# Cross attention with 16 heads: maxima rows issued by ScalarE, key side by half heads of two pairs, value products alternating between column halves, context loads one group nearer

## The chip, the core and the metric

The kernel runs on one core of one Trainium2 chip. The core has five engines that run side by side and meet only at semaphores: TensorE (PE; matmuls), VectorE (DVE), ScalarE (ACT), GpSimd (POOL) and SyncE (SP; here it only starts transfers). Transfers run on 16 DMA engines. The metric is the device time of one execution in microseconds; the median of three runs counts.

## The reference

`x` and `ctx_1024` are 128 batches of 64 rows of 128 numbers. One layer is computed, all of it in float32:

```
x = x + xattn(layernorm(x), ctx, ctx)
      q, k, v = rows @ W.T + b, 16 heads of 8 numbers
      scores  = q . k / sqrt(8), softmax over the 64 keys, times v, then @ Wo.T + bo
x = x + ffn(layernorm(x))
      two gates (out, in): grouped conv of 4 columns, batch norm over all 8192 rows, gelu, linear to 128,
      softmax, the 32 largest of 128 kept
      out = (x @ W) * gate_out + (x * gate_in) @ W + bias
```

## The kernel before

**Two phases.** The batch norm needs all rows, so the kernel first does the attention and the grouped convolution of everything (phase 1), and then the gates' top 32 and the two products (phase 2, 16 groups, VectorE busy nearly throughout). The change touches phase 1 and the start.

**Phase 1** works on 16 groups of 4 pairs of batches. It is a software pipeline: in step t of the loop `for t in range(FIRST, LAST + 1)` (t from -3 to 17), each engine works on group t+3 (layer norm), t+2 (keys and queries projected), t (row maxima), t-1 (softmax and value products, output projection) and t-2 (residual, second layer norm, convolution). Each engine has its own hand-written list for one step; they are coupled by counting semaphores.

**Scores with 96 rows.** A float32 score is computed as a bf16 matmul over 2 x 48 rows: q and k are split in three bf16 parts (`split_queries` on VectorE, `split_keys` on GpSimd), written to DRAM (`write_parts`, L228, 4 transfers a group) and read back stacked (`stack`, L240, 12 transfers a group, into `kst` and `qst`).

- `query_side` (L338) multiplies with the queries on the output rows; VectorE takes the maxima over the keys (`row_max`, L678). 16 heads in 8 calls a group; its matmuls alternate between the two column halves of the array (64 columns of weights each).
- The maxima are split in two bf16 parts, turned by PE (`turn_max`, L351), copied by ACT (`max_out`, L544, into `mT`), and written by a transfer into four more rows of `qst` (`max_rows`, L247). There are two such transfers a group, one for each half hp (two pairs).
- `key_side` (L291) multiplies again with the keys on the output rows, over 100 rows, so the maximum is already subtracted; ACT takes the exponential (`exp_half`, L511) into `pT`. It can only start when the maxima rows of its half have landed. Before, a call is one pair p with all 16 heads, 8 into each of two PSUM banks.
- `values` (L305) takes `pT` as weights (128 x 64 float32) and 18 columns of V with a column of ones. Each float32 matmul shows as two passes in the trace, so one call is 32 passes. Before, a call is one pair p, and all 32 passes go to the column half pp = p % 2.

**SP's list of one step, before:** `max_rows(t-1, 1)`; load x of t+5; load the context of t+4 (L205), which waits until PE has used the buffer, that is until `values_in(t)` (L373) is done; then wait for all key sides of t-1 and issue `stack(t+1)` for keys and queries (L240); write the parts of the keys of t+2; `max_rows(t, 0)`; write the parts of the queries of t+2. SP is a strict list: what stands behind a wait is late with it.

## Time and profile before

| | us |
|---|---|
| median of 3 runs | 907.33 (898.88 to 907.83) |
| profiled execution | 896.31, its span 894.5 |
| PE busy / weight loads | 642.7 / 509.5 |
| VectorE busy | 469.2 |
| ScalarE busy | 362.1 |
| GpSimd busy | 283.8 |
| mean granted TensorE clock | 0.608 of full speed |

Phase 1 ends near 650 us. In the page's 40 slices PE is busy six to nine tenths over most of phase 1, VectorE two to four; from slice 29 on VectorE stands at nine. How to read it: a step's length in phase 1 is the distance between the first key-side matmuls of two neighbouring groups. "Idle before" names who ended an engine's wait.

### The profile page before, as it was taken

What the parts mean: (1) busy time and instruction counts of PE and PEld (TensorE: products, weight loads), DVE (VectorE), ACT (ScalarE), POOL (GpSimd) and SP (SyncE); (2) the same over time, 40 slices, a digit from 0 to 9 for tenths busy, and PEclk for the clock granted to TensorE, in tenths of its full rate; (3) what the DMA queues carried; (4) which work ended last, traced back from release to release, by engine and by line L of the source; (5) the groups of instructions that cost most, each with busy time, mean ns of one, the idle gap of its engine ahead of it and who ended that gap; (6) DMA issues with size and microseconds to landing.
All of it is one profiled execution on the core that took longest, in us unless ns stands there. A gap on an engine that the chain in (4) does not pass through costs nothing.

```text
span 894.5 us, 15479 instructions
## 1 busy us (share of the span) xinstructions
PE 642.7 (72%) x5186; PEld 509.5 (57%) x5186; DVE 469.2 (52%) x2214; ACT 362.1 (40%) x995; POOL 283.8 (32%) x352
## 2 busy tenths in 40 slices
PE   2348695976969788796976999999466666575742
PEld 0126584765847566585755778887345545454531
DVE  7241333423334233323423354432399999999993
ACT  2213232323424234232323443333576565656563
POOL 4522031230302303031230321000135656565665
PEclk9655567657766557556666696656555555555555
DMA  5751506426164251605326344400000000000000
GB/s 119 167 103 39 122 23 118 75 58 115 31 118 66 67 95 39 131 14 119 62 59 117 59 77 87 73 2 2 1 1 25 12 25 12 25 13 24 22 15 25
DMA packets 64942, 52.70 MB, mean 59 GB/s; under 512 B 6805, under 2 KB 57174, under 8 KB 63318
## 3 DMA queue, kind: packets, MB, share of 16 engines
q1 hardware_dynamic: 64862, 51.70, 28.0%
q8 instruction: 42, 0.69, 0.3%
q14 instruction: 38, 0.31, 0.1%
HBM read 34.38 MB, written 16.78 MB: 57 GB/s over the span
## 4 chain that ended last, share of the span: by engine, by line
PE 40%; DVE 27%; DMA 13%; SPq 12%; issue 3%; ACT 3%; POOL 1%; POOLq 0%; ACTq 0%; DVEq 0%
PE ps_pv L305 15%; DVE kst L790 14%; DMA qst<-mT 12%; SPq L240 10%; DVE top_next L781 8%; PE ps_col L291 6%; PE ps_row L338 5%; PE ps_proj L373 3%; PE ps_proj L366 3%; DVE top_first L781 3%; PE ps_proj L360 2%; PE ps_mix L324 2%; SPq L228 1%; ACT gates L606 1%; DMA qst<-q_scratch 1%
## 5 line engine op out<-in xcount | busy, mean ns | idle before, releaser
L305 PEld LDWEIGHTS ps_pv<-vx,pT 128*64 128x64 f32 x2048 | 180.0, 186 | 18.5 <-issue 17.4
L305 PE MATMUL ps_pv<-vx,pT 128*64 128x18 f32 x2048 | 181.7, 243 | 0.2 <-DVE attn L696 0.2
L678 DVE TENSOR_REDUCE m<-ps_row 128x8 f32<-128x512 f32 x128 | 85.5, 690 | 174.9 <-PE ps_row L338 174.6
L803 POOL TENSOR_SCALAR ve<-ag 128x4 f32<-128x4 f32 x32 | 7.3, 227 | 454.9 <-DVE ag L670 453.8
L511 ACT ACTIVATE pT<-ps_col 128x512 f32<-128x512 f32 x128 | 69.5, 594 | 182.3 <-PE ps_col L291 181.5
L291 PE MATMUL ps_col<-qst,kst 100*128 100x64 bf16 x1024 | 60.5, 226 | 98.8 <-DMA qst<-mT 96.8
L291 PEld LDWEIGHTS ps_col<-qst,kst 100*128 100x128 bf16 x1024 | 50.8, 125 | 111.0 <-DMA qst<-mT 100.2
L790 DVE MATCH_REPLACE8 kst<-top_next,kst 128x128 f32<-128x128 f32 x384 | 101.1, 280 | 0.0
L338 PE MATMUL ps_row<-kst,qst 96*64 96x128 bf16 x1024 | 80.2, 297 | 9.5 <-DMA qst<-q_scratch 8.5
L338 PEld LDWEIGHTS ps_row<-kst,qst 96*64 96x64 bf16 x1024 | 55.0, 140 | 42.5 <-issue 25.8
L781 DVE MAX8 top_next<-kst 128x8 f32<-128x128 f32 x384 | 78.1, 279 | 0.0
L704 DVE TENSOR_TENSOR xr<-xr,ps_mix 128x256 f32<-128x256 f32 x32 | 13.4, 420 | 111.1 <-PE ps_mix L324 111.1
L485 PE MATMUL ps_proj<-wf_sb,x2T 128*128 128x128 f32 x128 | 33.2, 441 | 49.1 <-ACT x2T L624 49.1
L485 PEld LDWEIGHTS ps_proj<-wf_sb,x2T 128*128 128x128 f32 x128 | 28.5, 328 | 55.5 <-ACT x2T L624 55.5
L692 DVE RECIPROCAL den<-ps_pv 128x32 f32<-128x32 f32 x32 | 11.5, 358 | 77.4 <-PE ps_pv L305 77.4
L618 ACT ACTIVATE kst<-kst,neg_max 128x128 f32<-128x128 f32 x128 | 39.1, 388 | 21.5 <-DVE kst L790 21.5
L495 PE MATMUL ps_pv<-idf,kst 128*128 128x128 f32 x64 | 17.9, 435 | 34.1 <-POOL kst L880 34.1
L500 PE MATMUL ps_mix<-wf_sb,q 128*128 128x128 f32 x128 | 33.2, 441 | 11.0 <-ACT q L643 11.0
L877 POOL TENSOR_TENSOR kst<-kst 128x1024 f32<-128x1024 f32 x16 | 37.7, 2358 | 4.1 <-ACT kst L618 4.1
L500 PEld LDWEIGHTS ps_mix<-wf_sb,q 128*128 128x128 f32 x128 | 28.5, 327 | 17.4 <-ACT q L643 17.4
L586 ACT ACTIVATE x2T<-ps_turn 128x512 f32<-128x512 f32 x16 | 9.6, 597 | 67.0 <-PE ps_turn L381 67.0
L324 PE MATMUL ps_mix<-wo_sb,attnT 128*128 128x128 f32 x128 | 35.3, 424 | 0.0
(97 smaller groups left out, 1186.6 us busy)
## 6 DMA issues: line engine op xcount, KB each, us to landing
k_scratch<-k_parts SPq DMA_DIRECT2D x32, 192.0 KB, 7.5
q_scratch<-q_parts SPq DMA_DIRECT2D x32, 192.0 KB, 5.6
kst<-k_scratch SPq DMA_DIRECT2D x32, 192.0 KB
qst<-q_scratch SPq DMA_DIRECT2D x32, 192.0 KB
xr<-in_x_dram SPq DMA_DIRECT2D x16, 256.0 KB, 3.0
cT<-in_ctxT_dram SPq DMA_DIRECT2D x16, 256.0 KB, 2.7
kst<-k_scratch SPq DMA_DIRECT2D x32, 128.0 KB
qst<-q_scratch SPq DMA_DIRECT2D x32, 128.0 KB
```

The costliest lines, as they stand in the source:

```text
L240: sp.dma_start(dst, src).then_inc(moved[s], 16)
L291: mm = pe.matmul(ps_col[b][:, hh, :], k_cols(s, KROWS, h, p), qst[s][0:KROWS, h, p * SEQ:(p + 1) * SEQ], start=True, stop=True)
L305: mm = pe.matmul(pv_flat[pp * SEQ:(pp + 1) * SEQ, h * 2 * VW:(h + 1) * 2 * VW], pT[:, half % PT_RING, h % (HEADS // 2), :], vx[s][:, p, h, ...
L324: mm = pe.matmul(ps_mix[:, pp * DIM:(pp + 1) * DIM], attnT[:, hp, pp, :], wo_sb[:, :], start=True, stop=True)
L338: mm = pe.matmul(ps_row[b % 2][pp * SEQ:(pp + 1) * SEQ, hh, :, :], qst[s][0:MROWS, h, p * SEQ:(p + 1) * SEQ], k_cols(s, MROWS, h, p), star ...
L485: mm = pe.matmul(ps_proj[:, p * DIM:(p + 1) * DIM], x2T[:, p * 128:(p + 1) * 128], wf_sb[:, :], start=True, stop=True)
L500: mm = pe.matmul(ps_mix[:, p * DIM:(p + 1) * DIM], xsT[:, p * 128:(p + 1) * 128], wf_sb[:, :], start=True, stop=True)
L511: act.activation(pT[:, b % PT_RING, :, :], ps_col[b % 2][:, :, :], ACT.Exp, scale=SCALE).then_inc(act_exp, 1)
L618: ins = act.activation(part, part, ACT.Exp, bias=neg_max[s][:, n:n + 1])
L678: dve.tensor_reduce(m32[:, b // 4, :, 4 * j:4 * j + 4].rearrange("q a h -> q h a"), ps_row[b % 2][:, :, :, :], AX.X, ALU.max).then_inc(dve ...
L781: ins = dve.max(top[:, n, :], src)
L790: ins = dve.match_replace(picked[s][:, p, cols], top[:, n, :], src, PICKED)
```

## The change

It has these parts:

1. `max_rows` leaves SP. The same transfer is issued by ACT in `max_out`, behind the copy, after two waits (key sides of group g-2 done, and its own copy written). So it goes through ACT's DMA queue.
2. SP loads the context of t+3 where it loaded that of t+4. The wait is then for `values_in(t-1)`, of the step before.
3. `key_side(g, hp, j)` and `values(g, hp, j)` take half the heads (j) of two pairs (pp = 0, 1). The banks `ps_col` and the order of exponentials follow. The number of matmuls is the same. In `values` the matmuls alternate between the two column halves.
4. The step's order on PE and ACT is rewritten for it; on VectorE `row_max(t, 0)` and `row_max(t, 1)` come earlier and `normalise(t-1, 1)` one row earlier.
5. Fills: `kst[0]` is cleared by VectorE and `kst[1]` by GpSimd before anything else, the row of ones in `gates` comes by a transfer of 32 KB and not from a VectorE fill, and GpSimd clears `vx` one step later, behind `split_keys(0)`.

```
             for t in range(FIRST, LAST + 1):
-                if there(t - 1):
-                    max_rows(t - 1, 1)
                 if 3 <= t + 5 < GROUPS:
                     load_x(t + 5)
-                if 2 <= t + 4 < GROUPS:
-                    load_ctx(t + 4)
+                if 2 <= t + 3 < GROUPS:
+                    load_ctx(t + 3)
...
-                if there(t):
-                    max_rows(t, 0)
...
+            def key_side(g, hp, j):
+                for pp in range(2):
+                    p = 2 * hp + pp
+                    wait(pe, act_exp, 8 * g + 4 * hp + 2 * j + pp - 1)
                     for hh in range(HEADS // 2):
-                        h = b * (HEADS // 2) + hh
+                        h = j * (HEADS // 2) + hh
...
+            def values(g, hp, j):
+                wait(pe, act_exp, 8 * g + 4 * hp + 2 * j + 2)
+                for hh in range(HEADS // 2):
+                    h = j * (HEADS // 2) + hh
+                    for pp in range(2):
+                        mm = pe.matmul(pv_flat[pp * SEQ:(pp + 1) * SEQ, h * 2 * VW:(h + 1) * 2 * VW],
+                                       pT[:, 2 * j + pp, hh, :], vx[s][:, 2 * hp + pp, h, :], start=True, stop=True)
...
                 act.activation(mT[:, hp, :], ps_mix[0:64, 0:64].bitcast(BF16), ACT.Copy).then_inc(act_mT, 1)
 
+                wait(act, pe_col, 8 * (g - 1))
+                wait(act, act_mT, 2 * g + hp + 1)
+                act.dma_start(qst[g % 2][MROWS:KROWS, :, hp * 128:(hp + 1) * 128], mT[:, hp, :]).then_inc(m_moved[hp][g % 2], 16)
...
             dve.memset(half_neg[:, :], -0.5).then_inc(dve_half, 1)
+            dve.memset(kst[0][:, :, :, :].bitcast(F32).rearrange("p h a t -> p (h a t)"), 0.0).then_inc(dve_zero, 1)
...
-                if t == FIRST:
-                    dve.memset(kst[1][:, :, :, :].bitcast(F32).rearrange("p h a t -> p (h a t)"), 0.0).then_inc(dve_zero, 1)
-                    dve.memset(gates[2 * GATES:2 * GATES + 1, :], 1.0).then_inc(dve_ones, 1)
...
+            pool.memset(kst[1][:, :, :, :].bitcast(F32).rearrange("p h a t -> p (h a t)"), 0.0).then_inc(gp_zero, 1)
```

SP's queue before, from the end of one early step into the next (the two transfers of the maxima rows are L247, what a row waits for stands in brackets):

```order
L228 DMA k_scratch<-k_parts 128x3x256 [waits k_moved1,gp_split]
L228 DMA k_scratch<-k_parts 128x3x256
L247 DMA qst<-mT 4x16x128 [waits act_mT]
L228 DMA q_scratch<-q_parts 128x3x256 [waits q_moved1,dve_split]
L228 DMA q_scratch<-q_parts 128x3x256
L247 DMA qst<-mT 4x16x128 [waits act_mT]
L201 DMA xr<-in_x_dram 128x512 [waits dve_ag1]
L205 DMA cT<-in_ctxT_dram 128x512 [waits pe_v]
L240 DMA kst<-k_scratch 24x16x256 [waits k_out1,pe_col]
L240 DMA kst<-k_scratch 16x16x256
```

The same place of SP's queue in the changed kernel (line numbers differ, L242 is the stack):

```order
L230 DMA k_scratch<-k_parts 128x3x256 [waits k_moved1,gp_split]
L230 DMA k_scratch<-k_parts 128x3x256
L230 DMA q_scratch<-q_parts 128x3x256 [waits q_moved1,dve_split]
L230 DMA q_scratch<-q_parts 128x3x256
L202 DMA xr<-in_x_dram 128x512 [waits dve_ag1]
L206 DMA cT<-in_ctxT_dram 128x512 [waits pe_v]
L242 DMA kst<-k_scratch 24x16x256 [waits k_out1,pe_col]
L242 DMA kst<-k_scratch 16x16x256
```

The two L247 are gone. The context row still waits on `pe_v`, for a count that is one lower.

PE's queue before, from the first key side of a step (L291 key side, L351 `turn_max`, L324 `out_proj`, L360 keys, L305 values, L338 query side, L366 queries):

```order
L291 MATMUL ps_col<-qst,kst 128x64 x16
L351 MATMUL ps_mix<-idb,m_parts 64x128
L291 MATMUL ps_col<-qst,kst 128x64 x16
L324 MATMUL ps_mix<-wo_sb,attnT 128x128 x2
L360 MATMUL ps_proj<-cT,wk_sb 128x512
L305 MATMUL ps_pv<-vx,pT 64x18 x16
L291 MATMUL ps_col<-qst,kst 128x64 x16
L338 MATMUL ps_row<-kst,qst 64x128 x8
L305 MATMUL ps_pv<-vx,pT 64x18 x16
L291 MATMUL ps_col<-qst,kst 128x64 x16
L338 MATMUL ps_row<-kst,qst 64x128 x8
L366 MATMUL ps_proj<-xnT,wq_sb 128x512
```

The same place in the changed kernel (L284 key side, L338 `turn_max`, L316 `out_proj`, L347 keys, L299 values, L330 query side, L353 queries):

```order
L284 MATMUL ps_col<-qst,kst 128x64 x16
L338 MATMUL ps_mix<-idb,m_parts 64x128
L316 MATMUL ps_mix<-wo_sb,attnT 128x128 x2
L347 MATMUL ps_proj<-cT,wk_sb 128x512
L284 MATMUL ps_col<-qst,kst 128x64 x16
L299 MATMUL ps_pv<-vx,pT 64x18 x16
L330 MATMUL ps_row<-kst,qst 64x128 x16
L284 MATMUL ps_col<-qst,kst 128x64 x16
L299 MATMUL ps_pv<-vx,pT 64x18 x16
L353 MATMUL ps_proj<-xnT,wq_sb 128x512
L284 MATMUL ps_col<-qst,kst 128x64 x16
L330 MATMUL ps_row<-kst,qst 64x128 x8
```

`out_proj` now stands directly behind `turn_max`, whose result ACT must have copied first; the last key side stands one projection of queries later than before; the first query side stands behind two key sides and one value product (three and one before).

ACT's queue around the second maxima copy in the changed kernel (L500 exponentials, L504 norm, L541 `attn_out`, L533 and L537 `max_out` and its transfer, L525 `values_out`); before, `max_out` stood ahead of `attn_out` and behind both norms, with no transfer:

```order
L500 ACTIVATE pT<-ps_col 128x512 [waits pe_pv,pe_col] x2
L504 ACTIVATE x2all<-xr,nm,rs 128x128 [waits gp_rs2]
L504 ACTIVATE x2all<-xr,nm,rs 128x128 x3
L541 ACTIVATE attnT<-ps_mix 128x2x2x64 [waits pe_attnT]
L533 ACTIVATE mT<-ps_mix 64x128 [waits m_moved00,pe_mT]
L537 DMA qst<-mT 4x16x128 [waits act_mT,pe_col]
L525 ACTIVATE vx<-ps_proj 64x64x8 [waits pe_pv,pe_v]
```

Behind the transfer stand `values_out`, the norm of t+3, and the rest of ACT's step.

## Rows read from the trace of the kernel before

**Rows 1.** The page, chain of work that ended last, shares by line.

```profile
PE ps_pv L305 15%; DVE kst L790 14%; DMA qst<-mT 12%; SPq L240 10%; DVE top_next L781 8%; PE ps_col L291 6%; PE ps_row L338 5%; PE ps_proj L373 3%; PE ps_proj L366 3%; DVE top_first L781 3%; PE ps_proj L360 2%; PE ps_mix L324 2%; SPq L228 1%; ACT gates L606 1%; DMA qst<-q_scratch 1%
```

**Rows 2.** Windows of steps 9, 12, 13, 14: length; PE, PEld, DVE, ACT, POOL busy; clock; DMA.

```profile
375.10:416.30 41.20, 34.44 (x293) 27.74 (x293) 13.77 (x41) 13.03 (x27) 8.13 (x13) 0.54 0.35 72
...
492.00:521.90 29.90, 27.52 (x292) 21.73 (x292) 13.16 (x41) 12.92 (x27) 8.11 (x13) 0.74 0.42 70
521.90:548.80 26.90, 26.52 (x288) 20.92 (x288) 11.30 (x31) 10.21 (x21) 6.41 (x9) 0.75 0.49 90
548.80:576.20 27.40, 26.61 (x286) 23.05 (x286) 11.76 (x32) 9.39 (x20) 2.93 (x5) 0.63 0.45 74
```

**Rows 3.** Waits: us in total, times, longest; the second is of SP's queue.

```profile
PE ps_col L291 <- DMA qst<-mT: 96.8, 13, 13.3
...
SPq L205 <- PE ps_proj L373: 220.3, 12, 21.6
```

**Rows 4.** Timeline of step 9: start, us, engine, line.

```profile
375.76 1.09 ACT L511 ACTIVATE pT<-ps_col 128x512 f32<-128x512 f32 x2 [6.47 <-PE ps_col L291]
...
396.79 0.27 ACT L544 ACTIVATE mT<-ps_mix 64x128 bf16<-64x128 bf16 x1 [0.76 <-PE ps_mix L351]
...
397.61 2.05 PE L373 MATMUL ps_proj<-wv_sb,cT 128*128 128x128 f32 x8
...
399.70 0.35 SPq L205 DMA_DIRECT2D cT<-in_ctxT_dram  x1
...
400.15 4.31 SPq L240 DMA_DIRECT2D kst<-k_scratch  x6
...
408.88 0.59 SPq L247 DMA_DIRECT2D qst<-mT  x1
...
416.29 1.04 PE L291 MATMUL ps_col<-qst,kst 100*128 100x64 bf16 x16 [6.74 <-DMA qst<-mT]
```

**Rows 5.** Timeline of step 12, in which no context is loaded.

```profile
504.43 4.32 SPq L240 DMA_DIRECT2D kst<-k_scratch  x6
...
512.25 0.95 SPq L247 DMA_DIRECT2D qst<-mT  x1
...
522.00 0.72 PE L291 MATMUL ps_col<-qst,kst 100*128 100x64 bf16 x16 [1.77 <-DMA qst<-mT]
```

**Rows 6.** Chain (start, us, what), then a window (last three: clock, DMA share, GB/s).

```profile
228.34 1.97 PE ps_pv L305 x32
...
230.97 0.56 PE ps_row L338 x8
...
380.24 3.53 PE ps_pv L305 x32
...
390.23 2.00 PE ps_proj L366 x2
392.24 1.05 PE ps_row L338 x15
...
228.30:230.30 2.00, 2.00 (x35) 1.97 (x34) 1.71 (x14) 0.69 (x1) 1.01 (x2) 1.00 0.08 26
```

**Rows 7.** Timeline of the start and of step 0.

```profile
5.53 3.47 DVE L738 MEMSET kst<- 128x4096 f32 x1 [0.80 <-DVE ag L670]
...
10.76 6.88 DVE L739 MEMSET gates<- 1x8192 f32 x1 [1.76 <-issue]
...
21.59 0.61 POOL L824 CAST k_parts<-k 128x512 bf16<-128x512 f32 x1
...
28.53 4.43 SPq L240 DMA_DIRECT2D kst<-k_scratch  x6
...
44.49 1.12 PE L338 MATMUL ps_row<-kst,qst 96*64 96x128 bf16 x16 [8.54 <-DMA qst<-q_scratch]
...
61.95 0.61 SPq L247 DMA_DIRECT2D qst<-mT  x1
...
70.20 1.04 PE L291 MATMUL ps_col<-qst,kst 100*128 100x64 bf16 x16 [13.32 <-DMA qst<-mT]
```

More of the change, by code:

```diff
@@ L38 @@
 WRITES = 16 * 2
+RESTS = 10
 def wait(eng, sem, value):
@@ L278, in k_cols @@
                 return kst[s][0:rows, h, :, :].rearrange("r a (m p) -> r (a m) p", p=PAIRS)[:, :, p]
-            def key_side(g, p):
+            def key_side(g, hp, j):
                 s = g % 2
-                if p % 2 == 0:
-                    wait(pe, m_moved[p // 2][s], 16 * (g // 2 + 1))
-                if g < 2 and p == 0:
+                if j == 0:
+                    wait(pe, m_moved[hp][s], 16 * (g // 2 + 1))
+                if g < 2 and hp == 0 and j == 0:
                     pe.wait_ge(rows_in, 32)
-                for b in range(2):
-                    wait(pe, act_exp, 8 * g + 2 * p + b - 1)
+                for pp in range(2):
+                    p = 2 * hp + pp
+                    wait(pe, act_exp, 8 * g + 4 * hp + 2 * j + pp - 1)
@@ L289, in key_side @@
                     for hh in range(HEADS // 2):
-                        h = b * (HEADS // 2) + hh
-                        mm = pe.matmul(ps_col[b][:, hh, :], k_cols(s, KROWS, h, p),
+                        h = j * (HEADS // 2) + hh
+                        mm = pe.matmul(ps_col[pp][:, hh, :], k_cols(s, KROWS, h, p),
                                        qst[s][0:KROWS, h, p * SEQ:(p + 1) * SEQ], start=True, stop=True)
                     mm.then_inc(pe_col, 1)
-            def values(g, p):
-                s, pp = g % 2, p % 2
-                wait(pe, act_exp, 8 * g + 2 * p + 2)
-                if p == 0:
+            def values(g, hp, j):
+                s = g % 2
+                wait(pe, act_exp, 8 * g + 4 * hp + 2 * j + 2)
+                if hp == 0 and j == 0:
@@ L299, in values @@
                     wait(pe, act_v, g + 1)
-                if pp == 0:
-                    wait(pe, dve_attn, 2 * g + p // 2)
-                for h in range(HEADS):
-                    half = 2 * p + h // (HEADS // 2)
-                    mm = pe.matmul(pv_flat[pp * SEQ:(pp + 1) * SEQ, h * 2 * VW:(h + 1) * 2 * VW],
-                                   pT[:, half % PT_RING, h % (HEADS // 2), :], vx[s][:, p, h, :], start=True, stop=True)
+                if j == 0:
+                    wait(pe, dve_attn, 2 * g + hp)
@@ L343, in turn_max @@
                 wait(pe, dve_m, 2 * g + hp + 1)
-                if hp == 0:
-                    wait(pe, act_mT, 2 * g)
-                    wait(pe, dve_x1, 2 * g - 2)
-                else:
-                    wait(pe, act_mT, 2 * g + 1)
-                    wait(pe, act_attnT, 2 * g)
+                wait(pe, act_attnT, 2 * g - 1 + hp)
                 pe.transpose(ps_mix[0:64, 0:64].bitcast(BF16), m_parts[:, hp, :, :, :].rearrange("q a x h -> q (a x h)"),
@@ L416, in _ @@
                 if d:
[L417 to L418 removed]
+                    key_side(t - 1, 0, 1)
+                    values(t - 1, 0, 0)
                 if c:
                     query_side(t, 0)
+                    query_side(t, 1)
                 if d:
[L422 to L425 removed]
+                    key_side(t - 1, 1, 0)
+                    values(t - 1, 0, 1)
                 if q:
                     queries(t + 2)
+                if d:
+                    key_side(t - 1, 1, 1)
                 if c:
                     query_side(t, 2)
+                if d:
+                    values(t - 1, 1, 0)
+                if c:
                     query_side(t, 3)
[L431 to L435 removed]
                 if d:
@@ L438, in _ @@
                 if c:
+                    query_side(t, 4)
+                if d:
+                    values(t - 1, 1, 1)
+                if c:
+                    turn_max(t, 0)
                     values_in(t)
@@ L441, in _ @@
                 if d:
-                    values(t - 1, 3)
                     out_proj(t - 1, 0)
@@ L572, in _ @@
                     norm(t - 2, [x2all[:, PAIRS * (t - 2) + p, :] for p in range(PAIRS)], rs2, nm2).then_inc(act_ln2, 1)
+                if d:
+                    attn_out(t - 1, 0)
+                if c:
+                    max_out(t, 0)
+                    values_out(t)
                 if n:
@@ L928, in layouts @@
         "lin_w": lin, "ident": np.eye(128, dtype=f),
-        "minus_rows": minus.reshape(KROWS - MROWS, -1),
+        "minus_rows": minus.reshape(KROWS - MROWS, -1), "ones_row": np.ones((1, TILES * 128), f),
     }
```

70 lines of the change are left out of this document (24 added, 46 removed).

## The prediction, made before the changed kernel ran

> **What bounds the kernel now.** The chain of waits comes first [rows 1]. It runs through PE's value products (15% of the span), through VectorE's top 32 (phase 2, untouched), and then through two things that are no arithmetic: the flight of the maxima rows (12%) and SP issuing the stack (10%). The list of waits says where that is felt: PE stood 96.8 us in 13 waits before the first key side of a group, for `qst<-mT` [rows 3]. The timeline of step 9 shows the loop [rows 4]. The maxima were copied at 396.8, but their transfer was issued at 408.88, 11.8 us later, because SP is a list. SP sat on the context load until `values_in` ended (399.70; such waits sum to 220.3 us in 12 steps [rows 3]), then issued 12 stack transfers from 400.15 and two writes, and only then the maxima rows. These landed at 416.2, 7.4 us after their issue, behind the stack. PE idled 6.74 us.
>
> The window table gives the price [rows 2]. Step 9 took 41.2 us with a clock of 0.54. Step 12 has no context to load: the stack began at 504.43, 12.4 us into the step and not 25 us (400.15 - 375.1), and the step took 29.9 us though the maxima rows still flew 9.7 us (512.25 to 521.95) and PE idled 1.77 [rows 5]. Step 13, with neither stall, took 26.9. Steps 1 to 11 go from 70.2 to 492.0 [rows 7, 2]: 38.35 us each. So about 10 us a step are queueing, and PE is nearly full without them.
>
> **Part 1, maxima rows and context (edits 1 and 2).** The loop falls apart in two. The rows of hp = 0 are issued by ACT some 0.6 us after their copy; behind that copy PE still has `values_in` and the step's tail. Before, the copy ended at 397.1 and PE's work at 416.29 - 6.74 = 409.5 [rows 4]: 12.5 us, of which one value product (3.5), one query side and one turn now stand ahead of it. That leaves about 8 us to fly. The flight is bounded by 0.6 us (its issue alone) and by the 7.4 to 9.7 us behind a whole stack; from a queue of its own I take less than 7, so no wait. The rows of hp = 1 have more than a value product and a projection to hide under. On ACT the wait and the issue (0.59 us, from SP's row [rows 4]; 0.95 at worst [rows 5]) come twice a step, ahead of `values_out` and of exponentials 2 and 3; ACT is busy 13 of 41 us [rows 2], so I price it at nothing. The context then is loaded a whole step ahead still.
>
> **The stack becomes the next thing to be late.** It starts when the last key side is done. That was 12.4 us into step 12; in the new order the queries' projection (2.0 [rows 6]), a query side (0.6) and a bubble (1, below) stand ahead of it too, less what the values save: about 14.7. It took 16.1 us in step 9 (400.15 to 416.2, an upper bound), 16.0 at the start (28.53 to 44.49 [rows 7]) and at most 17.5 in step 12. So it lands at 30.8 to 32.2. The first query side of the next step comes some 7.3 us into it, at 34.5 for a step of 27.2. The cover is 2 to 4 us.
>
> **Part 2, alternating value products (edit 3).** A pass costs 3.53 / 32 = 110 ns at the low clock of step 9 and 1.97 / 32 = 62 ns at full clock [rows 6]. The nearest alternating row is L338, 64 columns of weights too, but bf16 and with 128 moving columns: 1.05 / 15 = 70 ns in the same low-clock step, less than a value pass with its 18. At full clock the same line takes 0.56 / 8 = 70 ns. I take 70 ns at the low clock, saving 128 x 0.040 = 5.1 us a step, and nothing at full clock. Bounds: no gain at all, and half of either (7.0 and 4.0 us). On this the Trainium skill, "TensorE: Matmul & The Clock Gate", section Part 3 (packing small matmuls), speaks against the edit: a weight load overlaps running matmuls only when the row groups differ, and here both halves use all rows. By that rule the gain is nil. The same page's 107 ns for 128 moving columns at 1.2 GHz speaks for it: 70 ns would be too short for halves taking turns. No row shows a float32 alternation.
>
> **Part 3, order.** `out_proj` behind `turn_max` must wait for ACT's copy, behind two exponentials (1.09 for both and 0.27 [rows 4]); the second key side no longer fills that. I charge 1 us a step. The earlier maxima on VectorE cost nothing: it is busy 13.8 of 41.2 us [rows 2].
>
> **Part 4, fills.** VectorE filled 3.47 + 6.88 us ahead of the statistics of group 1; GpSimd's split of the keys of group 0 therefore began at 21.59, and the first query side at 44.49, after a wait [rows 7]. Now 3.47 us stand at the very start, before x has landed, and cost the first statistics some 0.9. At most 9.4 us are won; I take 8.4, with a microsecond for the keys' own chain. The 32 KB of ones are hidden behind everything up to step 0. In step 0, PE idled 13.32 us for maxima rows issued at 61.95; with ACT issuing at once I leave 0.6 of it. Together 21 us.
>
> **The sum.** Without stalls a step takes S at the low clock and F at full clock. Step 9 gives S = 41.2 - 6.7 = 34.5. Step 13 at 0.75 spent half its time at either: 13.45 / 34.5 is 0.39 of the work, so F = 13.45 / 0.61 = 22. After: S = 34.5 - 5.1 + 1 = 30.4, F = 23. At a clock of 0.75 that is 26.2 us, at 0.63 (step 14) 28.1; I take 27.2. Steps 1 to 11: 421.8 - 299.2 = 122.6. Step 12: 2.7. Steps 13 to 16, which had no such stall: 6 in all. Start: 21. Sum 152, from the profiled 896.3: 744. The profiled run lies 11 us under the median of three (907.3), which spread over 9 us; I put the median at 748.
>
> **Rivals.**
> - A, alternation gives nothing: S = 35.5, F = 23, a step of 29.5 (a third at full clock). 12 x 2.3 + 7 more: 783. For it: a pass spends its time on weights, and its 18 columns are few. Against: the alternating line costs 70 ns with seven times the columns.
> - B, the maxima rows stay behind the stack although another queue issues them: they land 7.4 to 9.7 us after issue, or with the stack at 31, and PE waits 0 to 3.7 us a step, say 2: 772. The Trainium skill, "DMA: Bandwidth & Descriptors", section "Issuing engines are not separate DMA queues", says that a second issuing engine only saves issue time, since all run on the same 16 DMA engines.
> - C, the stack lands late: each microsecond beyond the 2 to 4 of cover costs 12 us in all; 3 beyond give 784.
> - D, better: alternation halves a pass at both clocks and PE, no longer idling, holds the clock higher: a step of 25 gives 720.
> - E, slower than before: ACT's issue blocks ACT. It decides from about 6 us for each of the two issues a step, when a step exceeds 38 us. SP's worst row here is 0.95 us.
>
> **How the numbers follow.** Forecast 0.45, A 0.17, B 0.13, C 0.10, D 0.13, E and whatever else ends within 1% or above 0.02. The forecast's own range is 730 to 768 (step 25.8 to 28.6). The asked range reaches to D and to A, B and C: 718 to 790. About 1% (9 us) is what a measurement can tell from no change; faster by more than that 0.97, within 0.01, slower 0.02.
>
> **What would show it.** Right: waits of PE for `qst<-mT` below 10 us in all; steps of 26 to 28.5 us; the stack issued about 15 us into a step; value calls of 2.2 us at the low clock; the first query side near 36 us and the first key side near 49. Wrong: PE waits for `qst<-mT` of 2 us a step (B); for `q_scratch` (C); value calls of 3.5 us at 0.5 clock (A); long idle on ACT around L537 (E). The forecast also fails if the clock stays near 0.5, since 30.4 a step gives 788.

## The result and the profile after

The changed kernel takes 707.83 us (median of 4 runs, 698.06 to 722.49) beside 903.11 for the kernel before on the same chip (4 runs, 896.0 to 907.83). The ratio of paired runs is 0.776, 95% interval 0.765 to 0.788: 22% faster. (The ratio leaves out runs in which the chip was disturbed, so it is not quite the quotient of the medians.) The forecast was 748 us with a range of 718 to 790, so the time lies 40 us under the forecast and 10 us under the range. The profiled execution has 702.76 us, with a span of 701.0.

The page of the changed kernel: span, granted clock in 40 slices, the chain of waits by line (as rows 1), and the groups of the value products and of the key side (busy us, mean ns of one, idle before it and its releaser):

```profile
span 701.0 us, 15492 instructions
...
PEclk9855698989898998898995666555555555555555
...
DMA qst<-mT 19%; DVE kst L784 17%; DVE top_next L775 10%; PE ps_pv L299 9%; PE ps_col L284 5%; PE ps_row L330 5%; PE ps_proj L353 3%; DVE top_first L775 3%; PE ps_proj L347 2%; ACT gates L599 2%; PE ps_proj L360 1%; ACT pT L500 1%; PE ps_mi
...
L299 PE MATMUL ps_pv<-vx,pT 128*64 128x18 f32 x2048 | 84.1, 228 | 0.5 <-ACT pT L500 0.5
...
L284 PE MATMUL ps_col<-qst,kst 100*128 100x64 bf16 x1024 | 53.6, 215 | 23.8 <-DMA qst<-mT 23.7
```

The clock reads 0.8 or more in slices 6 to 21 (about 88 to 368 us), and 0.5 to 0.6 in slices 3 to 5, in the last steps of phase 1 and in phase 2. SP's issue of the stack, 10% of the chain in [rows 1], has all but gone from it (all that SP issues is 1%). The value products fell from 15% of the chain to 9%. The flight of the maxima rows (from the issue of a transfer to its landing) rose from 12% to 19% of a shorter chain, yet PE waits for them only 23.7 us in all; it waited 96.8 [rows 3]. A transfer that lies on the chain is not the same as an engine that idles: PE does other work during most of each flight.

PE's waits in the changed kernel (us in total, times, longest):

```profile
PE ps_col L284 <- DMA qst<-mT: 23.7, 18, 3.1
...
PE ps_mix L316 <- ACT mT L533: 15.3, 15, 1.2
...
PE ps_row L330 <- DMA qst<-q_scratch: 9.4, 3, 7.7
```

The windows of steps 1 to 11, of the kernel before and then of the changed one (length; PE, PEld, DVE, ACT, POOL busy; clock; DMA share; GB/s); the changed one's are followed by its steps 7 and 8:

```profile
70.20:492.00 421.80, 336.33 (x3202) 268.19 (x3202) 148.10 (x433) 139.70 (x291) 85.96 (x135) 0.63 0.38 77
```

```profile
53.67:318.05 264.38, 232.40 (x3202) 178.56 (x3203) 150.89 (x439) 136.76 (x291) 87.62 (x139) 0.85 0.61 121
199.90:225.60 25.70, 21.90 (x292) 16.59 (x292) 15.48 (x41) 12.84 (x28) 8.10 (x13) 0.80 0.61 124
225.60:245.80 20.20, 18.69 (x292) 14.67 (x293) 13.05 (x41) 11.84 (x26) 8.14 (x13) 1.00 0.60 126
```

Eleven steps went from 38.35 to 24.03 us each, 157.4 us in all. PE's idle time in them fell from 85.5 to 32.0 us (421.8 - 336.3; 264.4 - 232.4). Its busy time fell by 103.9 us for the same 3202 matmuls. So two thirds of the gain are matmuls that take less time, by cheaper passes and by the higher clock together, and only a third is waits that went. The rest of the 193.5 us between the two spans: the start 16.5 (first key side at 53.67, was 70.20 [rows 7]), steps 12 to 15 14, the tail of phase 1 5.6. Phase 2 did not move: from PE's first product for the gates (447.73, was 641.26) to the end it takes 253 us in both.

The timeline of the changed kernel's step 7 shows the new loop (start, us, engine; x32 is one call of value passes):

```profile
199.90 0.72 PE L284 MATMUL ps_col<-qst,kst 100*128 100x64 bf16 x16 [0.58 <-DMA qst<-mT]
...
201.36 0.27 ACT L533 ACTIVATE mT<-ps_mix 64x128 bf16<-64x128 bf16 x1
...
201.71 0.56 ACTq L537 DMA_DIRECT2D qst<-mT  x1
201.77 0.74 PE L316 MATMUL ps_mix<-wo_sb,attnT 128*128 128x128 f32 x4 [0.98 <-ACT mT L533]
202.09 0.45 SPq L206 DMA_DIRECT2D cT<-in_ctxT_dram  x1
...
211.06 4.27 SPq L242 DMA_DIRECT2D kst<-k_scratch  x6
...
211.41 1.08 PE L299 MATMUL ps_pv<-vx,pT 128*64 128x18 f32 x32
...
216.79 0.58 ACTq L537 DMA_DIRECT2D qst<-mT  x1
...
225.61 0.72 PE L284 MATMUL ps_col<-qst,kst 100*128 100x64 bf16 x16 [1.21 <-DMA qst<-mT]
```

ACT issues the transfer of the second half 0.08 us after its copy ends (201.36 + 0.27 = 201.63, issue at 201.71). The first half's, issued 11.8 us after its copy in [rows 4], goes out at 216.79, 0.09 us after its copy, and lands when the last key side shown starts. The context load is issued 2.2 us into the step and holds nothing up. The stack starts 11.2 us into the step. Before it was 25 us [rows 4]. A value call takes 1.08 us where a call of as many passes took 1.97 at full clock [rows 6].

### The profile page after: what moved, and what is told of

Read it like the earlier page. It is cut to its first block, busy times and chain, and to the rows that moved or that the text cites. A ratio compares the mean times of both kernels' runs of the same rounds, so it can differ in the third digit from the quotient of the medians.

```text
span 701.0 us, 15492 instructions
## 1 busy us (share of the span) xinstructions
PE 510.6 (73%) x5186; PEld 393.6 (56%) x5186; DVE 467.7 (67%) x2213; ACT 359.4 (51%) x995; POOL 284.3 (41%) x352
## 4 chain that ended last, share of the span: by engine, by line
DVE 34%; PE 31%; DMA 20%; ACT 8%; issue 4%; POOL 1%; SPq 1%; POOLq 0%; ACTq 0%; DVEq 0%
DMA qst<-mT 19%; DVE kst L784 17%; DVE top_next L775 10%; PE ps_pv L299 9%; PE ps_col L284 5%; PE ps_row L330 5%; PE ps_proj L353 3%; DVE top_first L775 3%; PE ps_proj L347 2%; ACT gates L599 2%; PE ps_proj L360 1%; ACT pT L500 1%; PE ps_mix L316 1%; PE ps_proj L375 1%; DMA qst<-q_scratch 1%
## 5 line engine op out<-in xcount | busy, mean ns | idle before, releaser
L671 DVE TENSOR_REDUCE m<-ps_row 128x8 f32<-128x512 f32 x128 | 87.7, 689 | 121.6 <-PE ps_row L330 121.3
L500 ACT ACTIVATE pT<-ps_col 128x512 f32<-128x512 f32 x128 | 69.3, 594 | 87.7 <-PE ps_col L284 87.6
L330 PE MATMUL ps_row<-kst,qst 96*64 96x128 bf16 x1024 | 78.8, 294 | 10.1 <-DMA qst<-q_scratch 9.4
L299 PE MATMUL ps_pv<-vx,pT 128*64 128x18 f32 x2048 | 84.1, 228 | 0.5 <-ACT pT L500 0.5
L299 PEld LDWEIGHTS ps_pv<-vx,pT 128*64 128x64 f32 x2048 | 81.0, 163 | 2.7 <-ACT pT L500 0.6
L284 PEld LDWEIGHTS ps_col<-qst,kst 100*128 100x128 bf16 x1024 | 49.6, 123 | 54.8 <-DMA qst<-mT 29.9
L284 PE MATMUL ps_col<-qst,kst 100*128 100x64 bf16 x1024 | 53.6, 215 | 23.8 <-DMA qst<-mT 23.7
L330 PEld LDWEIGHTS ps_row<-kst,qst 96*64 96x64 bf16 x1024 | 49.5, 129 | 26.5 <-issue 11.9
L316 PE MATMUL ps_mix<-wo_sb,attnT 128*128 128x128 f32 x128 | 29.0, 362 | 15.3 <-ACT mT L533 15.3
L867 POOL TENSOR_SCALAR neg_max<-top_first 128x4 f32<-128x4 f32 x32 | 7.1, 222 | 78.9 <-DVE top_first L775 78.9
L640 ACT ACTIVATE k<-ps_mix,rsum 128x128 f32<-128x128 f32 x64 | 18.2, 367 | 34.6 <-PE ps_mix L489 34.6
L800 POOL TENSOR_TENSOR rs<-ve,half_neg 128x4 f32<-128x4 f32 x32 | 33.2, 1037 | 5.4 <-ACT xn L504 0.7
```

The costliest lines, as they stand in the source:

```text
L284: mm = pe.matmul(ps_col[pp][:, hh, :], k_cols(s, KROWS, h, p), qst[s][0:KROWS, h, p * SEQ:(p + 1) * SEQ], start=True, stop=True)
L299: mm = pe.matmul(pv_flat[pp * SEQ:(pp + 1) * SEQ, h * 2 * VW:(h + 1) * 2 * VW], pT[:, 2 * j + pp, hh, :], vx[s][:, 2 * hp + pp, h, :], sta ...
L316: mm = pe.matmul(ps_mix[:, pp * DIM:(pp + 1) * DIM], attnT[:, hp, pp, :], wo_sb[:, :], start=True, stop=True)
L330: mm = pe.matmul(ps_row[b % 2][pp * SEQ:(pp + 1) * SEQ, hh, :, :], qst[s][0:MROWS, h, p * SEQ:(p + 1) * SEQ], k_cols(s, MROWS, h, p), star ...
L500: act.activation(pT[:, b % PT_RING, :, :], ps_col[b % 2][:, :, :], ACT.Exp, scale=SCALE).then_inc(act_exp, 1)
L671: dve.tensor_reduce(m32[:, b // 4, :, 4 * j:4 * j + 4].rearrange("q a h -> q h a"), ps_row[b % 2][:, :, :, :], AX.X, ALU.max).then_inc(dve ...
```

## The experiments

Each kernel differs from the changed kernel ("after") or from the kernel before in the lines shown. Times are medians; ratios are to the kernel before as it ran beside them on the same chip, with medians of 897.5, 899.2, 895.9 and 894.7 us. "Step" (the mean length), "PE busy" and "clock" are those of steps 1 to 11 of each profiled run, in us and as a share of full speed.

| kernel | what it is | us | ratio [95%] | step | PE busy | clock |
|---|---|---|---|---|---|---|
| before | | 903.1 | 1 | 38.4 | 336.3 | 0.63 |
| b_rows | before + rows on ACT | 815.5 | 0.908 [0.901, 0.915] | 32.0 | 309.1 | 0.71 |
| b_ctx | before + context nearer | 772.2 | 0.860 [0.854, 0.867] | 27.9 | 290.1 | 0.77 |
| b_both | before + both | 768.1 | 0.856 [0.848, 0.863] | 28.0 | 296.9 | 0.75 |
| b_alt | b_both + alternation | 701.2 | 0.782 [0.777, 0.787] | 23.8 | 237.2 | 0.82 |
| b_alt_fills | b_alt + new fills | 693.8 | 0.772 [0.767, 0.777] | 22.8 | 225.5 | 0.87 |
| after | all, new order | 707.8 | 0.776 [0.765, 0.788] | 24.0 | 232.4 | 0.85 |
| rows_on_sp | after, rows on SP | 768.0 | 0.851 [0.845, 0.857] | 29.7 | 271.6 | 0.68 |
| ctx_t4 | after, context t+4 | 777.0 | 0.866 | 30.5 | 258.5 | 0.69 |
| v_grouped | after, runs of 16 passes | 753.0 | 0.843 [0.837, 0.850] | 26.6 | 268.2 | 0.84 |
| v_by_four | after, runs of 8 | 737.5 | 0.824 | 27.1 | 261.1 | 0.78 |
| v_by_two | after, runs of 4 | 695.5 | 0.768 [0.762, 0.775] | 24.4 | 233.5 | 0.86 |
| fills_old | after, old fills | 708.4 | 0.787 [0.779, 0.795] | 24.6 | 241.2 | 0.80 |
| keys_first | after, keys ahead of `out_proj` | 704.7 | 0.787 | 24.5 | 243.5 | 0.79 |
| spread | after, rows in 4 transfers | 757.0 | 0.845 | 27.7 | 254.4 | 0.76 |
| both_new | keys_first + spread | 731.3 | 0.816 | 24.6 | 229.8 | 0.87 |
| all_three | both_new + v_by_two | 733.3 | 0.819 | 25.9 | 238.0 | 0.84 |

A ratio without an interval is that of the medians; the runs behind it spread too much, or are too few, for an interval, so differences of one or two per cent between such rows say nothing.

### Undoing one part of the changed kernel

**v_grouped: the alternation.** The value products of one pair's eight heads run before the other's, so a column half gets 16 passes in a row.

```
-                for hh in range(HEADS // 2):
-                    h = j * (HEADS // 2) + hh
-                    for pp in range(2):
+                for pp in range(2):
+                    for hh in range(HEADS // 2):
+                        h = j * (HEADS // 2) + hh
                         mm = pe.matmul(pv_flat...
```

> The changed kernel, but in a value call the 8 heads of one pair come first and then the 8 heads of the other: the same matmuls in the same places, only not alternating between the column halves. Theory (the halves run side by side and alternation alone halves a pass): a call of 32 passes goes back from 1.1 to 2.0 us at full clock and from 1.9 to 3.5 us at half clock, VectorE and ScalarE unchanged, PE's value passes busy 84 -> about 165 us, and a step goes from 24.0 to about 28.5 us, since the clock falls too: 765 us in all. Rival (the regrouping by half heads or the missing stalls shortened the calls): calls stay near 1.1 us and the time stays within 1% of 705.

Measured 753.0 us, 0.843 against 0.776. The chain of waits of v_grouped (start, us, calls; some of a call's passes are not in the records), two calls of a step at the low clock, then two at full clock:

```profile
137.97 2.81 PE ps_pv L299 x29
...
143.00 3.13 PE ps_pv L299 x32
...
167.15 1.59 PE ps_pv L299 x29
...
170.49 1.76 PE ps_pv L299 x32
```

At full clock 1.59 us for 29 passes and 1.76 for 32 are 55 ns; the changed kernel has 1.08 / 32 = 34 ns in the call shown above. The whole group of value passes is busy 145.0 us for 84.1. So the alternation saves time at full clock too, where the forecast gave it nothing. A run of 16 already is cheaper than a run of 32 (62 ns [rows 6]).

**v_by_two and v_by_four: how long may a run be?** The half changes every 2 or 4 heads and not every head (4 and 8 passes in a row).

```
-                for hh in range(HEADS // 2):
-                    h = j * (HEADS // 2) + hh
-                    for pp in range(2):
+                for h2 in range(HEADS // 4):
+                    for pp in range(2):
+                        for hh in (2 * h2, 2 * h2 + 1):
+                            h = j * (HEADS // 2) + hh
...
```

(v_by_four: `HEADS // 8` and `range(4 * h2, 4 * h2 + 4)`.)

> The changed kernel with the value matmuls alternating every two heads (four passes to one column half, four to the other). If the halves only overlap at a change of half, the gain shrinks with the number of changes: a call about 1.5 us at full clock, near 725 us. If each half has a queue of work of its own that PE can look ahead into, a call stays at 1.1 us and the time at 705.

> The changed kernel with the value matmuls changing the column half every four heads (eight passes). Measured so far: 31 ns a pass with runs of 2 and of 4 passes, 51 with runs of 16, 62 with runs of 32. Theory (PE works ahead on the other half over some 5 or 6 passes around each change): runs of 8 give 35 to 40 ns a pass, a call of 1.15 to 1.3 us at full clock, about 715 us. Rival (a fixed cost for each run of passes in one half that only short runs hide): 31 ns as with 4, 705 us.

v_by_two took 695.5 us, the same as the changed kernel as far as the intervals tell, and nearly all its calls at full clock take 0.93 to 1.06 us in the chain of waits, for 0.90 to 1.04. That is the expectation's case in which PE works ahead on the other half. v_by_four took 737.5. Its calls in the chain of waits, at the low and then at full clock:

```profile
142.55 2.01 PE ps_pv L300 x29
...
146.78 2.33 PE ps_pv L300 x32
...
174.46 1.18 PE ps_pv L300 x29
...
177.39 1.35 PE ps_pv L300 x32
```

That is 69 to 73 ns a pass at the low clock and 41 to 42 at full clock: between v_by_two and v_grouped, as expected. The group of value passes, as the page of v_by_four gives it:

```profile
L300 PE MATMUL ps_pv<-vx,pT 128*64 128x18 f32 x2048 | 110.3, 233 | 0.5 <-ACT pT L501 0.5
```

It is busy 26 us more than in the changed kernel (84.1). The runs of v_by_four spread from 722.4 to 742.1 us. The shortest is 24 us above the shortest of the changed kernel (698.1), which is about what the passes explain; the longer ones, the profiled run (740.8) among them, are no evidence that anything else was lost.

**rows_on_sp: the queue of the maxima rows.** Everything else stays; SP's list gets `max_rows(t - 1, 1)` first and `max_rows(t, 0)` ahead of the queries' write, as before.

```
+                if there(t - 1):
+                    max_rows(t - 1, 1)
                 if 3 <= t + 5 < GROUPS:
                     load_x(t + 5)
...
+                if there(t):
+                    max_rows(t, 0)
                 if there(t + 2):
                     write_parts(t + 2, q_parts, ...)
...
                 act.activation(mT[:, hp, :], ..., ACT.Copy).then_inc(act_mT, 1)
...
-                act.dma_start(qst[g % 2][MROWS:KROWS, :, ...], mT[:, hp, :]).then_inc(...)
```

> The changed kernel with both transfers of the maxima rows issued by SP at the places they had before (behind the stack and the keys' write, and at the head of the next step). Theory (ScalarE's queue matters because the rows are issued when they are ready): the rows of the first half are issued some 3 to 5 us later in each step and land beside the tail of the stack; PE waits 3 to 4 us a step for them: about 745 us. Rival (a transfer flies as long from either queue and the earlier stack is what helped): the issue is late by no more than 1 us and the time is within 1.5% of 705.

Measured 768.0 us. PE's wait rose from 23.7 to 65.7 us. The timeline of rows_on_sp, from the stack to the next key side (L249 is the transfer, L294 the key side, L543 the copy), and its waits:

```profile
218.62 4.31 SPq L242 DMA_DIRECT2D kst<-k_scratch  x6
...
222.98 2.34 SPq L242 DMA_DIRECT2D qst<-q_scratch  x6
...
224.29 0.27 ACT L543 ACTIVATE mT<-ps_mix 64x128 bf16<-64x128 bf16 x1 [1.97 <-PE ps_mix L348]
...
225.79 0.93 SPq L230 DMA_DIRECT2D k_scratch<-k_parts  x2
...
226.84 0.61 SPq L249 DMA_DIRECT2D qst<-mT  x1
...
235.13 1.04 PE L294 MATMUL ps_col<-qst,kst 100*128 100x64 bf16 x16 [3.40 <-DMA qst<-mT]
```

```profile
PE ps_col L294 <- DMA qst<-mT: 65.7, 15, 6.8
```

The rows are ready at 224.56 and issued at 226.84, behind the stack and the write of the keys. 2.3 us in a list are enough for a wait of 3.4 us, since the changed kernel's slack is about nothing (0.6 and 1.2 us of waiting at the two steps shown above). Of the 62.3 us that steps 1 to 11 grew by, 23 are PE's idle time (55.1 for 32.0) and 39 are busy time at a lower clock (0.68 for 0.85).

**ctx_t4: the context as far ahead as before.**

```
-                if 2 <= t + 3 < GROUPS:
-                    load_ctx(t + 3)
+                if 2 <= t + 4 < GROUPS:
+                    load_ctx(t + 4)
```

> The changed kernel with the context load for group t+4 again, so SP waits for the values' projection of step t ahead of the stack. Theory (the stack's start sets the step as soon as the maxima rows have a queue of their own): the stack is issued 7 us later, 18 us into the step, lands 10 us into the next one, and PE waits 4 to 5 us a step for q_scratch rows: about 755 us. Rival (with the rows gone from SP the context's wait hides): within 1% of 705.

Measured 777.0 us. The timeline of ctx_t4 and its waits:

```profile
108.76 0.34 SPq L206 DMA_DIRECT2D cT<-in_ctxT_dram  x1
...
109.20 4.37 SPq L242 DMA_DIRECT2D kst<-k_scratch  x6
...
125.51 1.13 PE L330 MATMUL ps_row<-kst,qst 96*64 96x128 bf16 x16 [6.41 <-DMA qst<-q_scratch]
```

```profile
PE ps_row L330 <- DMA qst<-q_scratch: 79.4, 14, 7.8
...
PE ps_col L284 <- DMA qst<-mT: 6.0, 4, 2.8
```

The stack again stands behind the context load; the maxima rows, on ACT's queue, do not. So the wait changes place: 79.4 us for the stack (9.4 in the changed kernel) and only 6.0 for the maxima rows. The stack took 16.3 us from its issue to PE's first use, as long as in [rows 4] and [rows 7]. That is rival C of the forecast (the stack lands late), which the nearer context keeps away.

**fills_old: the fills.** The diff of part 5 in reverse.

> The changed kernel with the fills as they were before (both kst fills and the row of ones in the first step, vx ahead of the first keys' split). Theory (fills set the start of the first stack): the first query side and the first key side come about 5 us later, everything behind keeps its length: 710 us. Rival (covered by other work): within 2 us of the changed kernel.

Measured 708.4 us, ratio 0.787 against 0.776; the intervals overlap. Its first key side starts at 58.5 us, the changed kernel's at 53.7: 4.8 us, 0.7% of the kernel. The fills are worth about that, which the times alone cannot show.

### Building the change up from the kernel before

b_ctx is the diff of ctx_t4 in reverse on the kernel before, b_rows the transfer on ACT's queue alone, b_both the two.

> The kernel before with only the context loaded one group nearer. Theory (the step without a context load, 29.9 us, is the model): the stack is issued 12 us into a step, the rows behind it land 1 to 3 us late, steps of about 30 us: 805 us. Rival (the rows' own queue is what counts): above 850.

> The kernel before with only the maxima rows issued by ScalarE. Theory (the stack, still 25 us into a step behind the context's wait, becomes the late one): PE waits for q_scratch rows instead of maxima rows, a step of 32 to 34 us: about 840 us. Rival (the rows alone were the stall): 785 us, as with both.

> The kernel before, with only the maxima rows issued by ScalarE and the context loaded one group nearer; order, value products and fills as before. Theory (the queueing was worth about 10 us a step and some 12 us in step 0, the rest of the gain is the value products): PE's waits for the maxima rows fall from 97 to under 25 us, value calls stay at 3.5 and 2.0 us, a step is 28 to 29 us: about 785 us. Rival (the stalls were paid back by PE's clock or by a late stack): above 820 us, with a new wait named in the list of waits.

The nearer context alone brings 127 us (899.2 to 772.2). The queue alone brings 84. Together they bring 131: in the slow loop they remove the same stall, and the queue adds 4 us, which is inside the interval. The waits of b_rows show that its loop still waited for the maxima rows (32.6 us) and hardly for the stack (10.6), where the expectation had put the wait on the stack. b_ctx came out 33 us better than expected: with the context out of the way PE waits 17.1 us for the rows although SP still issues them (7.5 in b_both). In the changed kernel the same transfer put back on SP's list costs some 60 us (rows_on_sp). The changed kernel's steps are shorter (24 us for 28) and its order on PE is another; no run separates the two.

**b_alt: the alternation on the old order.** The values of two pairs are merged into one call of 64 passes that changes half with every head; order, key side and fills stay those of before.

```
-            def values(g, p):
...
-                wait(pe, act_exp, 8 * g + 2 * p + 2)
...
+            def values(g, hp):
...
+                wait(pe, act_exp, 8 * g + 4 * hp + 4)
...
                 for h in range(HEADS):
-                    half = 2 * p + h // (HEADS // 2)
...
+                    for pp in range(2):
+                        half = 2 * pp + h // (HEADS // 2)
...
-                    values(t - 1, 1)
...
-                    values(t - 1, 2)
+                    values(t - 1, 1)
...
-                    values(t - 1, 3)
```

> The kernel before with the maxima rows from ScalarE, the context one group nearer, and the value products of two pairs merged into one call of 64 passes that alternates between the column halves; the rest of the order and the fills as before. Against b_both (768 us, steps of 28.0, clock 0.75): theory (alternation alone gives the 50 us): a call of 64 passes takes 2.0 us at full clock, steps of 23 to 24 us, about 705 us. If it also raises the clock, the mean in steps 1 to 11 goes above 0.80. Rival (the new order of half heads was needed, by covering waits or by keeping the clock up): above 735 us with the clock still near 0.75.

> b_alt with the fills of the changed kernel: the first query side 5 us earlier than in b_alt and the time 5 us lower, about 700 us, which would be the changed kernel's time without its new order of key side and values.

The window of steps 1 to 11 and the group of value passes, of b_both, then of b_alt; then the window alone of b_alt_fills:

```profile
62.90:370.62 307.72, 296.85 (x3203) 239.37 (x3204) 148.56 (x431) 137.44 (x290) 85.82 (x135) 0.75 0.52 104
```

```profile
L295 PE MATMUL ps_pv<-vx,pT 128*64 128x18 f32 x2048 | 163.6, 232 | 0.2 <-DVE attn L690 0.2
```

```profile
61.65:323.65 262.00, 237.15 (x3202) 178.02 (x3202) 149.42 (x432) 139.38 (x291) 86.04 (x136) 0.82 0.62 121
```

```profile
L294 PE MATMUL ps_pv<-vx,pT 128*64 128x18 f32 x2048 | 79.8, 229 | 4.8 <-ACT pT L498 4.1
```

```profile
57.31:308.50 251.19, 225.50 (x3202) 171.18 (x3202) 154.25 (x433) 139.21 (x291) 86.13 (x136) 0.87 0.63 126
```

b_both to b_alt is the cleanest pair of the study. It changes the order of the value passes and, with it, the places of two calls; the busy time of the same 2048 passes falls from 163.6 to 79.8 us, and the kernel goes from 768.1 to 701.2. The group's idle time grows by 4.6 us, since a merged call waits for two exponentials more. b_alt_fills adds only the fills and takes 693.8 us. It has neither the half-head key side nor the new order of the steps, and is as fast as the changed kernel (0.772 [0.767, 0.777] and 0.776 [0.765, 0.788]). Those two parts have no worth of their own that these runs can show.

### Trying to take the last waits away

**keys_first** puts `keys(t + 2)` ahead of `out_proj(t - 2, 1)`, to fill the bubble (PE's idle time ahead of `out_proj`) of part 3 of the prediction. **spread** sends the maxima rows as four transfers of one row each (the waits for them then count 64 and not 16):

```
-                act.dma_start(qst[g % 2][MROWS:KROWS, :, hp * 128:(hp + 1) * 128], mT[:, hp, :]).then_inc(...)
+                for r in range(4):
+                    act.dma_start(qst[g % 2][MROWS + r:MROWS + r + 1, :, hp * 128:(hp + 1) * 128],
+                                  mT[16 * r:16 * (r + 1), hp, :]).then_inc(...)
```

**both_new** has the two, **all_three** v_by_two besides.

> The changed kernel with the keys' projection ahead of out_proj on PE. PE waited 15.3 us in 15 times for ScalarE's copy of the maxima ahead of out_proj; the projection covers that. Theory (the 1 us a step is real cost): the wait is gone and the time falls by 10 to 18 us, to about 690 us. Rival (the maxima rows' landing sets the step anyway, and it is not moved): the wait for qst<-mT grows by as much, within 1% of 705.

> The changed kernel with each transfer of maxima rows issued as four, one per destination row (16 source partitions and 16 heads each, so that it may use 16 DMA engines and not the 4 that 68 packets a transfer point to). Theory (the flight of 4 to 10 us is the share of four engines that are busy with the stack): flights fall to 2 to 5 us, PE's 23.7 us of waits for them to under 8: about 690 us. Rival (the flight is waiting behind the stack's packets on whatever engines, and ScalarE pays three more issues of 0.56 us twice a step): flights as long, 705 to 725 us.

> Both edits, keys ahead of out_proj and the maxima rows in four transfers each. If both theories hold: 680 us. If only the first holds: 690 to 700.

> Both edits and the value matmuls alternating every two heads, which measured the same as every head or up to 1% less: 675 to 690 us, and the same as both_new within 1% if the alternation's grain costs nothing.

keys_first: the wait for ACT's copy fell from 15.3 to 3.3 us, and the one for `qst<-q_scratch` rose from 9.4 to 16.2; `qst<-mT` stayed (24.4). The stack starts no later than before (8.4 to 14.6 us into a step, 9.2 to 13.6 in the changed kernel), but the query side that needs it comes about 1 us earlier (4.1 to 4.4 us into a step for 5.0 to 5.2, its wait left out). PE's idle time in steps 1 to 11 fell by 5.7 us, its busy time rose by 11 at a clock of 0.79 for 0.85, and the time is that of the changed kernel within the scatter (703.9 to 719.7). The bubble was real, but closing it brought nothing that these runs can show. spread: ACT's queue in its timeline shows a price:

```profile
204.82 2.45 ACTq L538 DMA_DIRECT2D qst<-mT  x4
```

Four issues take 2.45 us, each 0.61, where one takes 0.56. Half of the 128 small transfers land within 2.9 us of their issue, but the flights on which PE waited are no shorter (3.4 to 10.6 us in the chain of waits; 2.3 to 9.7 in the changed kernel). PE waits 40.5 us for the rows, and 13.7 us (5.2 in the changed kernel) for ACT's copy ahead of the convolution. Steps 1 to 11 of the profiled run are 40 us longer than the changed kernel's: 18 us of idle time and 22 of busy time at a clock of 0.76 for 0.85. 757 us lies outside both expectations. The two other kernels that contain the edit wait as long for the rows (36.8 and 41.7 us) and missed their 680 and 675 to 690 us by about 50.

## Why the prediction was right or wrong

**The loop through the queues: right.** The rows on ACT's queue go out 0.1 us after the copy, the context holds nothing, and without the alternation the kernel is where the forecast's own sums put it. b_both has no change but the two; steps of S = 34.5 and F = 22 at its clock of 0.75 give 26.9 us, plus its 1.0 us of idle time a step 27.9; measured 27.97. Rival A, the kernel whose alternation brings nothing, was put at 783, and b_both, which has no alternation at all and the old fills, took 768. (By the forecast's formula rival A's step is 29.4 us at a clock of 0.69; a third of the time at full clock, as its sum says, would give 30.1.) Rival E did not show: an issue takes ACT's queue 0.56 us in the median and 1.14 at most.

**Value passes: this term failed.** The step was "I take 70 ns at the low clock ... and nothing at full clock". What was measured, beside it:

| passes in a row to one half | 32 | 16 | 8 | 4 | 2 |
|---|---|---|---|---|---|
| ns a pass, full clock | 57 to 62 | 50 to 55 | 36 to 42 | 29 to 34 | 28 to 33 |
| ns a pass, low clock | 104 to 110 | 90 to 98 | 63 to 73 | 53 to 58 | 51 to 57 |

(The kernels are before, v_grouped, v_by_four, v_by_two, after; from their calls in the chain of waits that lie at one clock throughout.) A pass was halved at both clocks. That saves 128 x 31 ns = 4.0 us a step at full clock and 128 x 53 ns = 6.8 at the low one, about what the forecast named as its bound (4.0 and 7.0). The alternation is worth 67 us (b_both to b_alt; 0.074 of 897 by the ratios), the rise of the clock from 0.75 to 0.82 between the two included. The forecast had given it 783 - 748 = 35. That difference, 32 us, is most of the 40 missed. The error was to take the query side's 70 ns as the price of any alternating row. That row moves 128 columns, and it takes 70 ns at either clock; nothing showed that a call with 18 columns would meet the same limit. It was an upper bound, and should have stood at the end of the range.

The Trainium skill, "TensorE: Matmul & The Clock Gate", section Part 3, says that a weight load overlaps running matmuls only when the row groups differ. All passes here use all the rows and differ in the column half alone, and they take half the time. By the rule the gain is nil, so the measured times disagree with it, and the measurement decides. The Trainium skill, "TensorEngine Tiling (Array Packing)", section Key Properties, says that different tiles can load weights and multiply in parallel; the halved time agrees.

**The clock: wrong, and the second reason.** I assumed 0.63 to 0.75. It was 0.85 in steps 1 to 11. By the forecast's own formula a step with F = 23 and S = 30.4 takes 27.1 us at 0.69 and 24.8 at 0.85; with the measured passes (F = 19.0, S = 28.7) it takes 24.0 and 21.2. So the clock alone was worth 2.3 us a step, the passes alone 3.1, and both 5.9. The kernel did not get all of that: it took 24.0. What PE's idle time beyond the bubble and an unexplained microsecond (both next) took back, 2.8 us, is about what the clock gave. So the 3.2 us by which a step was forecast too long are as many as the passes alone explain; that the two other errors nearly cancelled is luck.

**Waits: rival B was partly right.** PE idled 32.0 us in steps 1 to 11, 2.9 a step. With the bubble taken out of F and S (it is idle time itself) a step at 0.85 is 20.1 us of work, with the idle time 23.0; the last 1.0 us to the measured 24.0 is not accounted for. The forecast said no wait for `qst<-mT`, below 10 us in all; it was 23.7. The flights in the chain of waits are 2.3 to 9.7 us with a median near 7.2 on ACT's own queue, and were 6.8 to 10.1 with a median near 8.2 on SP's; rows_on_sp, the changed kernel with SP's queue, has 5.3 to 9.0 and 8.1. I had taken less than 7. The cover was as forecast: in step 7 the rows were issued at 216.79 and landed at 225.61, 8.8 us later, of which PE idled 1.21 and worked 7.6, for the 8 forecast. The Trainium skill, "DMA: Bandwidth & Descriptors", section "Issuing engines are not separate DMA queues", says that another issuing engine saves the issue time only; flights of nearly the same length from either queue agree. What it saves is not small all the same: the place in SP's list, 11.8 us in [rows 4].

**The stack: right, and earlier than forecast.** 11.2 us into step 7 (9.2 to 13.6 in steps 1 to 11) for 14.7 forecast, because the values and the whole step shrank; PE waited for it 9.4 us, 7.7 of them at the start.

**The bubble of `out_proj`: right.** 15.3 us in 15 waits is the 1 us a step that was charged. keys_first shows no gain from closing it.

**The start: too good.** The first query side came at 39.42 (forecast 36) and the first key side at 53.67 (forecast 49). 16.5 us of 21 were won. The fills brought about 5 us, not 8.4: the first statistics started 1.6 us later (5.07 for 3.44) and not 0.9, and the last section shows what took most of the rest. In step 0 PE still waited 2.38 us for the maxima rows, 0.6 forecast.

**The likeliest case.** Rival D, "halved passes and a higher clock", 720 us at 0.13, is nearest to what happened, and it was still 12 us too slow: it had steps of 25 us for the 24.0 measured, and steps 12 to 15 and the tail gave 19.6 us where 8.7 were counted; cheaper passes work there too. The sum in the profile is -4.5 (start), +34.8 (steps 1 to 11), +10.9 (the rest): 41 us.

## What to carry to other kernels

Where small matmuls use half of the array's columns, let consecutive ones change the half, every one or two products: it halved their time here at both clocks, and b_alt had it with nearly the old order. A transfer on which a loop depends must not stand in a list behind a load that is needed a step later; first bring that load nearer, then move the transfer to a queue of its own, and count on the saved place in the list and not on a faster flight. When a price isn't in the trace, the nearest row is one end of the range: ask which of its properties makes it cost what it does before it becomes the value.

## What the runs showed of the hardware

**Length of a run.** The table above: at full clock the time per pass falls from about 60 to about 31 ns as the run in one column half shrinks from 32 to 4, and stays there at 2. It reads as if PE got ahead with the other half while one is busy, with a run of 4 short enough. That is a reading of the durations and not shown; no row tells the load of one half beside the pass of the other.

**The clock follows more than the alternation.** In steps 1 to 11 it was 0.63 before, 0.75 to 0.77 without the stalls (b_both, b_ctx), 0.82 in b_alt, 0.84 in v_grouped with dear passes, 0.85 after, 0.87 in b_alt_fills; 0.68 and 0.69 where a stall comes back. PE's idle time does not order them: b_both idled 10.9 us in steps 1 to 11 and had 0.75, keys_first 26.2 and 0.79, the changed kernel 32.0 and 0.85. So neither the alternation nor fewer waits alone explain the clock, and what sets it here stays open.

**VectorE is held up beside GpSimd.** Timelines of the changed kernel, at the start and in step 7:

```profile
16.50 1.15 POOL L824 TENSOR_TENSOR k_parts<-k_rest,k_parts 128x512 bf16<-128x512 f32 x1
...
16.78 3.15 DVE L704 CAST q_parts<-q 128x512 bf16<-128x512 f32 x1 [7.63 <-ACT q L515]
17.59 2.06 POOL L837 MEMSET vx<- 128x1152 f32 x2
...
24.79 0.43 DVE L704 CAST q_parts<-q 128x512 bf16<-128x512 f32 x1 [1.69 <-ACT q L515]
```

```profile
213.60 1.16 POOL L824 TENSOR_TENSOR k_parts<-k_rest,k_parts 128x512 bf16<-128x512 f32 x1
...
213.73 1.06 DVE L677 CAST m_parts<-m 128x32 bf16<-128x32 f32 x1
214.72 1.26 POOL L810 TENSOR_TENSOR xr<-xr,bo_row 128x512 f32<-128x512 f32 x1
214.83 1.19 DVE L679 TENSOR_TENSOR m_parts<-m,m_parts 128x32 bf16<-128x32 f32 x1
...
216.08 0.31 PE L338 MATMUL ps_mix<-idb,m_parts 128*64 128x128 bf16 x1 [1.29 <-DVE m_parts L679]
...
223.72 0.18 DVE L677 CAST m_parts<-m 128x32 bf16<-128x32 f32 x1
...
223.94 0.19 DVE L679 TENSOR_TENSOR m_parts<-m,m_parts 128x32 bf16<-128x32 f32 x1
```

The cast of 0.43 us took 3.15. It began beside GpSimd's split of the keys (to 17.65) and ended at 19.93, 0.3 us after GpSimd's fill of `vx` (to 19.65). So about 2 of its 2.7 us too many stand beside the fill that the change had moved there, on the chain of the first queries. With the 0.7 us of the first statistics they come near the 3.6 us by which the fills fell short (8.4 forecast, 4.8 measured). In step 7 a cast of 0.18 us takes 1.06 and ends 0.03 us after GpSimd's subtraction, and the next instruction, of 0.19, takes 1.19 and ends 0.04 us after GpSimd's addition; PE waited 1.29 us for them, and the maxima rows left that much later. The Trainium skill, "SBUF — State Buffer", section "Who interferes with whom", says that the two engines share a pair of ports and that, when VectorE runs in a two-port mode, the one that comes second blocks for the other's whole instruction; the ends of the two casts agree. No kernel here took one of these overlaps away, so what they cost the whole is argued from the rows and not shown.
